# Three small bias tiles move in the on-chip memory: from ahead of the attention tiles to behind them

## The reference

```
x = x + layernorm(attention(layernorm(x)))
x = x + layernorm(mlp(layernorm(x)))

attention: q, k, v = x @ W + b      16 heads of 128, D = 256, biases b_Q, b_K, b_V
           scores = q k^T / sqrt(128), causal, softmax
           out = sum over heads of z @ W_O + b_O
mlp:       gate, up = x @ Wg, x @ Wu      2048 wide, weights of 4 bits with a scale per 32
           out = (gelu_tanh(gate) * up) @ Wd
```

## The kernel before

| tiles, in their order | address of the first | address modulo 1024 |
|---|---|---|
| stream, x_res, xnT, wqk, wv, wo, mask, w_raw | 17056 | 672, each of them |
| bias_q, bias_k, bias_v (64 bytes each) | 169632 | 672, 736, 800 |
| bias_o, x_in, qT, kT, q_early, k_early, v, v_late, probs, pT, turned, back, zT | 169824 | 864, each of them |
| nmax, sums, rsum, words, scale, w4 and the like | 225120 | various |

## Time and profile before

### The profile page before, as it was taken

How to read it: one execution, slowest core, us unless ns; L and a number is a source line. 1 busy time by engine, 2 the same in 40 slices (tenths; PEclk the granted TensorE clock), 3 DMA queues, 4 the chain that set the end, 5 groups by cost and what they waited for, 6 DMA issues and landing times.

```text
span 1580.0 us, 28430 instructions
## 1 busy us (share of the span) xinstructions
PE 1557.7 (99%) x9600; PEld 1397.5 (88%) x9600; DVE 1061.7 (67%) x3074; ACT 974.6 (62%) x2433; POOL 712.4 (45%) x1069
## 2 busy tenths in 40 slices
PE   7999999999999999999999999999999999999998
PEld 5889898889998999899889999998888888888887
DVE  5666677677777777677767766766666666666665
ACT  6886677777676777776767776644444444444443
POOL 6773455445454555454545544333333333333333
PEclk9999999999999999999999999999999999999999
DMA  4653434434444344433443444471000010000000
GB/s 140 191 165 110 131 129 136 150 129 136 141 148 131 129 145 141 142 128 128 146 143 122 144 161 146 148 270 41 27 14 27 14 41 28 14 28 14 27 16 25
DMA packets 157440, 167.69 MB, mean 106 GB/s; under 512 B 15856, under 2 KB 130672, under 8 KB 157296
## 3 DMA queue, kind: packets, MB, share of 16 engines
q1 hardware_dynamic: 157296, 165.89, 32.4%
HBM read 94.53 MB, written 71.30 MB: 105 GB/s over the span
## 4 chain that ended last, share of the span: by engine, by line
PE 86%; ACT 4%; DMA 4%; DVE 3%; SPq 1%; issue 1%; POOL 0%; DVEq 0%; POOLq 0%
PE fbank L715 14%; PE fbank L716 14%; PE fbank L717 14%; PE obank L717 7%; PE obank L716 7%; PE obank L715 7%; PE ubank L715 5%; PE ubank L716 5%; PE ubank L717 5%; PE ubank L739 3%; PE fbank L817 3%; DMA turned_scratch<-turned 2%; DMA back<-turned_scratch 1%; ACT probs L609 1%; SPq L510 1%
## 5 line engine op out<-in xcount | busy, mean ns | idle before, releaser
L715 PE MATMUL fbank<-xnT_hi,wqk_hi 128*128 128x512 f32 x768 | 302.2, 394 | 1.0 <-DVE xnT_lo L893 1.0
L716 PE MATMUL fbank<-xnT_lo,wqk_hi 128*128 128x512 f32 x768 | 301.2, 392 | 0.0
L717 PE MATMUL fbank<-xnT_hi,wqk_lo 128*128 128x512 f32 x768 | 300.8, 392 | 0.0
L1261 POOL TENSOR_TENSOR pT_lo<-back,pT_hi 128x512 fp32r<-128x512 f32 x128 | 166.2, 1298 | 278.3 <-ACT pT_hi L677 278.3
L620 ACT ACTIVATE w_raw<-fbank 128x512 f32<-128x512 f32 x128 | 76.5, 598 | 254.4 <-PE fbank L717 254.4
L1223 POOL TENSOR_SCALAR probs<-probs,rsum 128x128 f32<-128x128 f32 (+1 forms) x512 | 209.1, 427 | 20.2 <-DVE rsum L916 17.1
L717 PEld LDWEIGHTS fbank<-xnT_hi,wqk_lo 128*128 128x128 f32 x768 | 144.9, 189 | 31.5
L908 DVE CUSTOM_DVE_ANT_0 probs<-ubank,mask 128x128 f32<-128x128 f32 (+1 forms) x512 | 154.9, 355 | 26.1 <-PE ubank L717 25.2
L715 PEld LDWEIGHTS fbank<-xnT_hi,wqk_hi 128*128 128x128 f32 x768 | 145.0, 189 | 24.4 <-DVE xnT_lo L893 1.4
L716 PEld LDWEIGHTS fbank<-xnT_lo,wqk_hi 128*128 128x128 f32 x768 | 145.0, 189 | 22.3
L997 DVE SCALAR_TENSOR_TENSOR w_raw<-w_raw,fbank 128x512 f32<-128x512 f32 x128 | 88.0, 687 | 104.1 <-ACT w_raw L620 102.3
(11 more groups left out here) (128 smaller groups left out, 4570.0 us busy)
## 6 DMA issues: line engine op xcount, KB each, us to landing
turned_scratch<-turned SPq DMA_DIRECT2D x128, 384.0 KB, 2.5
back<-turned_scratch SPq DMA_DIRECT2D x512, 96.0 KB, 2.2
w_raw<-in_w_pairs SPq DMA_DIRECT2D x28, 256.0 KB, 3.3
w_hi_scratch<-w_hi SPq DMA_DIRECT2D x48, 128.0 KB, 2.0
w_lo_scratch<-w SPq DMA_DIRECT2D x48, 128.0 KB, 2.0
x_res<-in_x SPq DMA_DIRECT2D x16, 256.0 KB, 2.9
wqk_hi<-w_hi_scratch SPq DMA_DIRECT2D x16, 256.0 KB, 4.6
wqk_lo<-w_lo_scratch SPq DMA_DIRECT2D x16, 256.0 KB, 5.2
```

The costliest lines, as they stand in the source:

```text
L715: nc.tensor.matmul(out, a[0], b[0], start=start, stop=False, skip_group_check=skip)
L716: nc.tensor.matmul(out, a[0], b[1], start=False, stop=False, skip_group_check=skip)
L717: return nc.tensor.matmul(out, a[1], b[0], start=False, stop=stop, skip_group_check=skip)
L1261: pool.tensor_tensor(lo[:].rearrange("p u b (a j) -> p (u b) a j", j=32), mem.back[m % 2][:, :, 0:2].rearrange("p a u b j -> p (u b) a j") ...
```

## The change

The three tiles of the biases of q, k and v are named behind `zT` and ahead of `nmax`. They are 192 bytes together. So every tile of the second group, bias_o to zT, lies 192 bytes lower and begins at 672 modulo 1024; the three bias tiles lie at 224928, 224992 and 225056, 54 times 1024 bytes above where they were (672, 736 and 800 modulo 1024 as before); all others stay. No engine's instructions change in number, order, shape or waits: on TensorE, VectorE, ScalarE, GpSimd and SyncE the rows of the two programs read the same, addresses apart.

```diff
@@ -218,9 +218,6 @@
         self.wo_p = [sb(f"wo_{s}", [P, HEADS, D], F32R) for s in ("hi", "lo")]
         self.mask = sb("mask", [P, SEQ])
         self.raw = sb("w_raw", [P, RAW, 2, D])
-        self.bias_q = sb("bias_q", [P, HEADS])
-        self.bias_k = sb("bias_k", [P, HEADS])
-        self.bias_v = sb("bias_v", [P, HEADS])
         self.bias_o = sb("bias_o", [P, D])
@@ -241,6 +238,9 @@
         self.turned = sb("turned", [P, 4, 3, 2, 32])
         self.back = [sb(f"back{i}", [P, 4, 3, 2, 32]) for i in range(2)]
         self.zT = [sb(f"zT_{s}", [P, CHUNK], F32R) for s in ("hi", "lo")]
+        self.bias_q = sb("bias_q", [P, HEADS])
+        self.bias_k = sb("bias_k", [P, HEADS])
+        self.bias_v = sb("bias_v", [P, HEADS])
         self.nmax = [[sb(f"nmax{i}{b}", [P, 2]) for b in range(2)] for i in range(2)]
```

## The result

| | before | after |
|---|---|---|
| median | 1585.75 us (9 runs, 1583.55 to 1588.39) | 1591.27 us (9 runs, 1589.76 to 1592.95) |
| profiled execution, its span | 1582.72, 1580.0 us | 1592.93, 1591.1 us |

The ratio is 1.0039, with an interval of 1.003 to 1.0048: slower, by 5.5 us between the medians. It is clear of the 0.2% that a measurement tells. The time lies in the stated range, but it is a change where none was forecast, on the side to which the prediction gave 0.17.

The account below looks back on a forecast made before the run. The prediction took TensorE's pace from product to product as the bound. All terms were taken as 0, a sum of 0 us, so it forecast 1585.5 us, no change (chance 0.62), with a range of 1578 to 1594 us.

Parts of the forecast that it names:

- the slower rival: All 4608 narrow products take on 2.5 ns more with stationary operands at 672: 11.5 us, 1597 us; chance 0.17.
- the prediction's own sign of being wrong: Mean lengths of the narrow groups moving by more than 1 ns, all or only those with a mixed pair before.
- What bounds the kernel: TensorE, busy 1557.7 of 1580.0 us at full clock with short waits; its pace from product to product sets the end.
- the 11 to 14 ns above the columns: TensorE products' cost beyond columns at 2.4 GHz: about 14 ns wide, 11 ns narrow; the only place for address effects.
- the products with operands of either group: Output and down projection, 3072 narrow products, going from 672 and 864 to 672 for both: 0, ends 3.1 us either way.
- a control: Scores and z, both operands already at 864, read 281 ns against the projections' 280 and 281: equal address worth 0.
- Scores and z: 1536 narrow products of the second group only, from 864 to 672 for both operands: 0, with 2.5 ns for the range.
- Wide products: 3840 products of 512 columns, operands unmoved, only neighbours in time shifted: 0, ends -6.9 and +6.9 us.
- Other engines and DMAs: Same operations at shifted addresses, differences under 1% and hidden behind TensorE's work: 0; 1.8 us on GpSimd if uncovered.
- The faster rival: Fewer collisions of TensorE's reads with other engines beside wide products: up to 6.9 us less, 1578.6 us; chance 0.21.

Follow-up runs that it names:

- gap_224: Kernel before with one 32-byte tile more ahead of the second group: stationary less moving address 224 instead of 192 in both projections; 1585.41 us, ratio 1.0001.
- gap_64: Changed kernel with bias_q alone left ahead of the second group, operand address difference 64 in the projections; 1589.98 us, ratio 1.0031 to the kernel before.
- wide_32: Kernel before with small tiles moved: wide q, k, gate, up at difference 32, v at 256, projections at 224; 1596.94 us, ratio 1.0079.
- tuned: Kernel before with small tiles moved to combine the best differences: wide 0, projections 224, scores -32, z 64; 1589.62 us, ratio 1.0031.
- sweep1: Kernel before with small tiles between large ones: down projection at differences 32 (kT) and 64 (v), output projection 128, wide 0; 1591.28 us, ratio 1.0053.
- all_up: Kernel before with the three bias tiles ahead of everything, so both groups stand at 864 modulo 1024; 1590.91 us, ratio 1.0029.

## Why the prediction was right where it was and wrong where it was

**The number** was right by the width of the range, not by its reasoning. 1591.3 us lies below 1594 us, and that end was set from the slower rival. The sum was 0 us and the measured change is 5.5; the prediction's own sign of being wrong, narrow means that move by more than 1 ns, has come.

**What bounds the kernel**: right. TensorE's pace set the result; clock and waits stayed. The layout had to act through the 11 to 14 ns above the columns, and did.

**The step that failed** is "I take 0" for the products with operands of either group. It rested on a control: scores and z, at an equal address, read 281 ns like the mixed pairs, so the equal address was said to be worth nothing. The control was no control. Scores, and half of z, are runs of three narrow products behind a float32 one, and the rows that I used hold the second and third. In after the scores still go at 117.8 ns from second to third at a difference of 0, where the long runs go at 120. The profile after shows how the run's length comes in: in the output projection the distances behind the first product have a median of 113 ns, behind the second 119, and 120 from the third on. These medians sum to 352 ns, those of before to 353; the loss begins after the first three. The other half of z follows the output projection without a break, which the prediction overlooked. There the three distances were 118.6, 117.5 and 115.9 ns before and are 120.0, 120.0 and 120.8 after, with a difference of 0 both times: three products at 0 behind a run at 192 were no measure of a run at 0. Why a run starts so isn't shown. Measured: 1.5 to 1.7 ns more per product inside runs, 5.1 us for the 3072 products with their borders, against bounds of 3.1 us either way.

**Scores and z**: taken at 0 with 2.5 ns for the range. They lost 3.0 us in the profiled executions, most of it at their borders, where the last product of z went from 117.7 to 123.4 ns and that of scores from 117.5 to 121.4. Inside, the half of z behind the output projection lost and the other half gained (119.7 to 117.5 ns from second to third), so that their mean hardly moved. I had no term for borders.

**Wide products**: taken at 0. They had +1.8 us in the MLP, inside the bounds of 6.9 us, and 0.2 us in the attention stage. The MLP's part repeats in every layout but before, also where the whole is no slower (gap_224), so it isn't due to a difference of 0; its cause is open.

**Other engines and DMAs**: right, 0 of both; the busy sums of the engines moved by 0.2% at most, and TensorE waited for no DMA.

**The rivals.** The slower one named the right groups, the right sign and the point from which it decides (0.7 ns a product), with a price of 11.5 us; 5.5 us came. The price itself was off: by the earlier trace rows the surplus is 14.2 ns for wide and 10.8 ns for narrow products, 3.4 ns apart and not 2.5, which makes 15.7 us and 1601 us. Its mechanism was wrong: it laid the surplus to operands at 672, and with everything at 864 the pace was the same. How the two operands lie to one another counts. It also argued from the wide products' larger surplus, and that has to do with width: for wide products a difference of 0 is a good one. The faster rival is dead: no time was gained, and the wide means into fbank and ubank stayed apart.

**The size** stays partly open. The MLP's 4.5 us are shown to be the layout's, 2.7 of them with the down projection's slower pace; the other 1.8, in the wide products, have no cause shown. With the medians' 5.5 us, some 1 us is left for the attention stage (3 us at the interval's upper end), while its narrow distances sum to 2.4 + 3.0 = 5.4 us more. That TensorE's waits for other engines there take up part of a slower pace is likely, but not shown. Why a difference of 128 is slow and 96 fast isn't explained by any run.

## What to carry to other kernels

Where a trace shows TensorE busy all through and the same products at slightly different paces, the addresses of the operands, one against the other, are a thing that an edit changes unasked: here 192 bytes of bias tiles were worth 0.4%, and in the wrong place 1.2%. Before taking a group of products as a control for another one, look whether its runs have the same length and the same neighbours. A layout should be judged by the whole time: the rule "equal addresses are good" held for wide products and failed for narrow ones, and four layouts with narrow projections as fast as before or faster (gap_224, gap_64, wide_32, tuned) did not beat the old one.

## What the runs showed of the hardware that was not expected

- The pace of back-to-back products at the full clock depends on how the operands' tiles lie to one another: 256 columns in the two projections 116.8 to 120.3 ns, 512 columns 226.7 to 233.6 ns. At a difference of 0, placing both 192 bytes higher changes nothing (0.1 ns), nor does moving one by 512 bytes. The difference alone is not a full key: at 224 the narrow pace was 116.8 ns in gap_224 and 117.8 in wide_32.
- The tile loaded next seems to matter as much as a product's own: the last wide product before a down projection went from 225.8 to 235.0 ns in gap_224, where its own operands had not moved, and in sweep1 it took 235.0 ns before kT and 225.9 before v.
- What ran before matters too: three products of z at an unchanged difference of 0 went from 117.3 to 120.3 ns on average as the output projection ahead of them went from 192 to 0. all_up gives the same 120.3 ns with z's tiles at the very addresses of before.
- The Trainium skill, on the page "TensorE: Matmul & The Clock Gate" (section "Step-by-step: what each phase is for"), states that loading the next weights takes no SBUF read bandwidth from the running product. The section has no term for addresses, and here the operands' addresses, one against the other, change the pace by up to 3% (116.8 to 120.3 ns). That the two streams meet in the memory is my reading of it; no run measured it by itself.
- In a stage where TensorE waits 0.2 us at most, two executions of the same program took 523.62 and 523.63 us.
